# Experts' gate, up and down products of a two-layer decoder in plain fp32 matmuls

## The reference, cut to what matters

```python
def _L1_ffn_ref(hidden_states, gate_w, Wg, Wu, Wd, sg, su, sd):
    ...
    x = hidden_states.reshape(-1, h)
    scores = jax.nn.sigmoid(x @ gate_w.T)
    topk_w, topk_ids = jax.lax.top_k(scores, K)
    topk_w = topk_w / topk_w.sum(-1, keepdims=True)
    comb = jnp.zeros((T, E), dtype=x.dtype).at[jnp.arange(T)[:, None], topk_ids].add(topk_w)
    g = jnp.einsum('th,ehi->tei', x, Wg)
    u = jnp.einsum('th,ehi->tei', x, Wu)
    eo = jnp.einsum('tei,eih->teh', jax.nn.silu(g) * u, Wd)
    routed = jnp.einsum('teh,te->th', eo, comb)
    shared = jax.nn.silu(x @ sg) * (x @ su) @ sd
    return (shared + routed).reshape(b, s, h)
```

## Time and profile before

| what | us |
|---|---|
| runs of the kernel, three | 1480.43, 1484.72, 1488.59; median 1484.72 |
| the profiled execution | 1483.09 |
| its span, first to last instruction | 1481.7 |
| TensorE busy in the span | 1232.3 (83%) |
| VectorE busy | 889.1 (60%) |
| ScalarE busy | 599.9 (40%) |
| GpSimd busy | 327.0 (22%) |

### The profile page before, as it was taken

One profiled execution on the slowest core, in us unless ns is written; L12 is line 12 of the kernel. 1 busy time (PEld: TensorE's weight loads), 2 busy tenths in 40 slices (PEclk: granted clock), 3 DMA queues, 4 the chain that ended last, 5 costly groups with the idle time before them and its releaser, 6 DMA issues.

```text
span 1481.7 us, 19507 instructions
## 1 busy us (share of the span) xinstructions
PE 1232.3 (83%) x7048; PEld 748.6 (51%) x7048; DVE 889.1 (60%) x2091; ACT 599.9 (40%) x1205; POOL 327.0 (22%) x327
## 2 busy tenths in 40 slices
PE   4568868976479934699999899898978999999998
PEld 2234645653336621243335333265544778777777
DVE  3676638575938575767675776177787575542322
ACT  2232146322255621356554465644435343232222
POOL 3410023220443220600000200033321232222222
PEclk9789998985889975799999999999997999999999
DMA  6144530360024300133322020060000000000000
GB/s 180 64 90 93 79 49 1 72 87 1 0 75 86 44 0 0 61 68 44 44 44 44 1 44 2 1 182 1 0 1 1 1 1 15 1 15 1 15 1 15
DMA packets 45919, 56.44 MB, mean 38 GB/s; under 512 B 8742, under 2 KB 30592, under 8 KB 45824
## 3 DMA queue, kind: packets, MB, share of 16 engines
q1 hardware_dynamic: 45824, 55.20, 18.6%
HBM read 40.37 MB, written 14.68 MB: 37 GB/s over the span
## 4 chain that ended last, share of the span: by engine, by line
PE 62%; DVE 22%; ACT 7%; issue 5%; POOL 2%; DMA 2%; SPq 0%; DVEq 0%; ACTq 0%; POOLq 0%
PE psum L923 12%; PE psum L940 7%; PE psum L814 5%; PE psum L602 5%; PE psum L784 4%; PE psum L833 4%; PE psum L684 3%; DVE mx L1639 3%; PE psum L709 2%; PE psum L695 2%; PE psum L503 2%; DVE stats L1254 2%; DVE small L1419 1%; PE psum L584 1%; PE psum L927 1%
## 5 line engine op out<-in xcount | busy, mean ns | idle before, releaser
L1639 DVE TENSOR_REDUCE mx<-psum 128x1 f32<-128x512 f32 (+3 forms) x384 | 200.1, 552 | 87.4 <-PE psum L787 63.1
L1865 POOL TENSOR_TENSOR work<-work,small 128x308 f32<-128x308 f32 x128 | 90.9, 713 | 312.6 <-DVE small L1435 312.6
L923 PE MATMUL psum<-H_r,area_r 128*128 128x512 f32 x408 | 145.6, 398 | 0.0
L1927 POOL TENSOR_TENSOR work_r<-work,work_r 128x512 fp32r<-128x512 f32 x68 | 89.3, 1313 | 250.1 <-ACT work_r L1214 250.1
L784 PE MATMUL psum<-stack_area 96*128 96x512 bf16 (+3 forms) x288 | 100.3, 353 | 45.9 <-DVE mx L1639 44.5
L1766 DVE TENSOR_TENSOR work<-work,psum 128x512 f32<-128x512 f32 x68 | 46.7, 687 | 150.3 <-PE psum L923 148.2
L1155 ACT ACTIVATE work<-psum 128x512 f32<-128x512 f32 (+1 forms) x192 | 94.7, 526 | 78.5 <-PE psum L836 59.9
L684 PE MATMUL psum<-area 128*128 128x308 f32 x256 | 100.7, 479 | 20.1 <-DVE work L1432 15.8
L1214 ACT CAST work_r<-work 128x512 fp32r<-128x512 f32 x68 | 42.2, 620 | 164.3 <-DVE work L1770 157.9
L1155 ACT ACTIVATE HT<-psum 128x384 f32<-128x384 f32 (+2 forms) x192 | 82.4, 454 | 47.6 <-PE psum L836 31.5
L833 PE MATMUL psum<-stack_area 98*128 98x512 bf16 (+3 forms) x288 | 94.9, 336 | 7.1 <-ACT work L1155 3.6
(11 more groups left out here) (254 smaller groups left out, 2721.5 us busy)
## 6 DMA issues: line engine op xcount, KB each, us to landing
stack_area<-parts_a0q SPq DMA_DIRECT2D x24, 128.0 KB, 4.2
stack_area<-parts_a0k SPq DMA_DIRECT2D x24, 128.0 KB, 7.0
stack_area<-parts_a1q SPq DMA_DIRECT2D x24, 128.0 KB, 4.6
stack_area<-parts_a1k SPq DMA_DIRECT2D x24, 128.0 KB, 7.2
stack_area<-parts_d0q SPq DMA_DIRECT2D x18, 128.0 KB, 4.3
stack_area<-parts_d0k SPq DMA_DIRECT2D x18, 128.0 KB, 7.1
stack_area<-parts_d1q SPq DMA_DIRECT2D x18, 128.0 KB, 4.1
stack_area<-parts_d1k SPq DMA_DIRECT2D x18, 128.0 KB, 6.7
```

The costliest lines, as they stand in the source:

```text
L923: done = pe.matmul(u.bank(x), w[:, c, :], h[:, c, cols], start=k == 0, stop=k == len(products) - 1)
L1639: dve.tensor_reduce(mx[:, j, t, half:half + 1], u.bank(k)[:, 0:cols], AX.X, ALU.max).then_inc(*u.empties(k))
L1865: pool.tensor_tensor(ex3, ex3, small[:, of_i + 4:of_i + 8].unsqueeze(2).to_broadcast([P, HPG, CTX]), ALU.mult).then_inc(ctx_prob, 1)
L1927: pool.tensor_tensor(work_r[x % 4][:, :], work[x % 4][:, :], work_r[4 + x % 4][:, :], ALU.subtract).then_inc(act_lo, 1)
```

## The change

Upper and lower parts go away. The gate and up products are one plain fp32 matmul for each half of the contraction, from the unsplit weights and the tokens in `HT`; the down product is one plain fp32 matmul for each tile of 128 tokens, from `work[y % 4]` and the unsplit weight. All three kinds of splits go, on ScalarE, VectorE and GpSimd, with their tiles' second names, their semaphores and the steps in the order of stages.

```diff
-            weave(e["context"](1, "e"), chain(e["context_out"](0, "e"), e["route"](0), e["split_first"]()))
+            weave(e["context"](1, "e"), chain(e["context_out"](0, "e"), e["route"](0)))
...
             def experts(b):
+                pe.wait_ge(*landed["moe"].all())
                 for n in range(SPANS):
...
-                    pe.wait_ge(tokens_lo[b], DC * (n + 1))
                     if n == 0:
+                        for pair in range(TILES // 2):
+                            pe.wait_ge(*u_ln["f", b].empty(pair))
                         pe.wait_ge(sel_done, 1)
...
                     for x in range(NE + DOWN_LAG):
                         if x < NE:
-                            if b == 0 and n == 0:
-                                pe.wait_ge(upper_lo, 3 * (x + 1))
-                            for u, name in ((of_g, "g"), (of_u, "u")):
-                                _, w_hi, w_lo = expert_weights(x, name)
+                            for u, w in ((of_g, wg), (of_u, wu)):
                                 pe.wait_ge(*u.vacant(x))
-                                products = [(w, h, c) for c in range(DC) for w, h in ((w_hi, hx_r[b]), (w_hi, HT_r[b]), (w_lo, hx_r[b]))]
-                                for k, (w, h, c) in enumerate(products):
-                                    done = pe.matmul(u.bank(x), w[:, c, :], h[:, c, cols], start=k == 0, stop=k == len(products) - 1)
+                                for c in range(DC):
+                                    done = pe.matmul(u.bank(x), w[:, c, x, :], HT[b][:, c, cols], start=c == 0, stop=c == DC - 1)
                                 done.then_inc(*u.fills(x))
...
                         if x >= DOWN_LAG:
                             y = x - DOWN_LAG
-                            _, w_hi, w_lo = expert_weights(y, "d")
...
-                            pe.wait_ge(act_lo, first + y + 1)
-                            lo, hi = work_r[y % 4], work_r[4 + y % 4]
+                            pe.wait_ge(*(of_sel.empty(y) if y < EXPERTS else of_u.empty(y)))
                             for q in range(TPS):
-                                obank, o = outs.bank(q // 2), q % 2
-                                for m, (part, w) in enumerate(((hi, w_hi), (hi, w_lo), (lo, w_hi))):
-                                    done = pe.matmul(obank[:, o * D:(o + 1) * D], part[:, q * P:(q + 1) * P], w,
-                                                     start=(y == 0 and o == 0 and m == 0), stop=(y == NE - 1 and m == 2), skip_group_check=True)
+                                done = pe.matmul(outs.bank(q // 2)[:, q % 2 * D:(q % 2 + 1) * D], work[y % 4][:, q * P:(q + 1) * P], down_weights(y),
+                                                 start=(y == 0 and q % 2 == 0), stop=y == NE - 1, skip_group_check=True)
                             done.then_inc(down_done, 1)
...
-                        act.copy(hx_r[b][:, c, cols], HT[b][:, c, cols]).then_inc(tokens_hi[b], 1)
...
-                    act.copy(upper, whole).then_inc(upper_hi, 1)
...
-                            act.activation(s[:, :], of_g.bank(x), ACT.Silu).then_inc(*of_g.empties(x))
-                            act.wait_ge(*(of_sel.empty(x) if x < EXPERTS else of_u.empty(x)))
-                            act.copy(hi[:, :], s[:, :]).then_inc(act_hi, 1)
+                            act.activation(work[x % 4][:, :], of_g.bank(x), ACT.Silu).then_inc(*of_g.empties(x))
...
-                        dve.tensor_tensor(HT_r[b][:, c, cols], HT[b][:, c, cols], hx_r[b][:, c, cols], ALU.subtract).then_inc(tokens_lo[b], 1)
...
-                    dve.tensor_tensor(lower, whole, upper, ALU.subtract).then_inc(upper_lo, 1)
...
-                            pool.wait_ge(act_hi, first + x + 1)
-                            pool.tensor_tensor(work_r[x % 4][:, :], work[x % 4][:, :], work_r[4 + x % 4][:, :], ALU.subtract).then_inc(act_lo, 1)
```

More of the change, by code:

```diff
@@ L186, in sb @@
             return ctx.enter_context(nc.sbuf_tensor(name, shape, dt))
[L188 to L191, removed]
         def sem(name):
@@ L203, in build @@
         X = sb("X", [P, BATCH * TILES, D])
[L204 to L208, removed]
+        H = [sb(f"H{b}", [P, TILES, D]) for b in range(BATCH)]
+        HT = [sb(f"HT{b}", [P, DC, SEQ]) for b in range(BATCH)]
+        stack_area = sb("stack_area", [P, 8192])
+        area = [sb(f"area{b}", [P, 9728]) for b in range(BATCH)]
+        work = [sb(f"work{i}", [P, SPAN]) for i in range(8)]
         W1 = sb("W1", [P, 2048])
-        W2, W2_r = sb2("W2", [P, 2048])
+        W2 = sb("W2", [P, 2048])
         consts = sb("const_tile", [P, KEPT_COLS])
@@ L284, in build @@
                 vx[phase, b] = carve(area[b], at + GROUPS * HPG * CTX, HEADS * STRIP).rearrange("p (h e) -> p h e", h=HEADS)
-        hx, hx_r = [[h[b][:, :, :].rearrange("p t d -> p (t d)").rearrange("p (c t) -> p c t", c=DC) for b in range(BATCH)] for h in (H, H_r)]
+        hx = [H[b][:, :, :].rearrange("p t d -> p (t d)").rearrange("p (c t) -> p c t", c=DC) for b in range(BATCH)]
         ox = [[hx[b][:, 0, :], hx[b][:, 1, :], HT[b][:, 0, :], HT[b][:, 1, :]] for b in range(BATCH)]
@@ L297, in build, with down_weights @@
         w_proj = carve(area[0], 9216, 512).rearrange("p (c n) -> p c n", c=DC)
-        wd_shared, wd_shared_r = [carve(a[0], 8144, D) for a in (area, area_r)]
-        wg, wg_r = [carve(a[0], 3792, DC * NE * INNER).rearrange("p (c e i) -> p c e i", c=DC, e=NE) for a in (area, area_r)]
-        wu, wu_r = [carve(a[1], 3792, DC * NE * INNER).rearrange("p (c e i) -> p c e i", c=DC, e=NE) for a in (area, area_r)]
+        wd_shared = carve(area[0], 8144, D)
+        wg = carve(area[0], 3792, DC * NE * INNER).rearrange("p (c e i) -> p c e i", c=DC, e=NE)
+        wu = carve(area[1], 3792, DC * NE * INNER).rearrange("p (c e i) -> p c e i", c=DC, e=NE)
         sel = carve(area[1], 8144, 1024, BF16).rearrange("p (e n) -> p e n", e=EXPERTS)
[L302 to L316, removed]
+        wd = carve(stack_area, 4096, EXPERTS * D).rearrange("p (e n) -> p e n", e=EXPERTS)
+        def down_weights(x):
+            return wd_shared if x == EXPERTS else wd[:, x, :]
         combt = [carve(area[b], 0, 512, BF16) for b in range(BATCH)]
@@ L385, in build @@
         values_zeroed = sem("values_zeroed")
-        comb_split, sel_done, upper_hi, upper_lo = sem("comb_split"), sem("sel_done"), sem("upper_hi"), sem("upper_lo")
-        tokens_hi, tokens_lo = per_batch("tokens_hi"), per_batch("tokens_lo")
-        act_hi, act_lo, down_done = [sem(f"expert_{n}") for n in ("hi", "lo", "down")]
+        comb_split, sel_done, down_done = sem("comb_split"), sem("sel_done"), sem("expert_down")
         dve_steps, act_steps, pool_steps = Steps(sem("dve_steps")), Steps(sem("act_steps")), Steps(sem("pool_steps"))
@@ L946, in tensor_engine @@
                           context=context, context_out=context_out, spline=spline_layer, attention_inputs=attention_inputs, maxima=maxima,
[L947 removed]
+                          weighted=weighted, masked_inputs=masked_inputs, route=route, experts=experts,
                           between=lambda where: None))
@@ L1179, in route @@
                     yield
-                for n in range(SPANS):
-                    for c in range(DC):
-                        cols = slice(n * SPAN, (n + 1) * SPAN)
-                        act.copy(hx_r[b][:, c, cols], HT[b][:, c, cols]).then_inc(tokens_hi[b], 1)
[L1184 to L1188, removed]
-                    act.copy(upper, whole).then_inc(upper_hi, 1)
[L1191 to L1197, removed]
             def experts(b):
                 for n in range(SPANS):
-                    of_g, of_u, of_sel = u_g[b, n], u_u[b, n], u_sel[b, n]
+                    of_g = u_g[b, n]
                     first = (b * SPANS + n) * NE
@@ L1204, in experts @@
                         if x < NE:
[L1205 to L1208, removed]
                             act.wait_ge(*of_g.full(x))
-                            if k >= 4:
+                            if first + x >= 4:
                                 act.wait_ge(down_done, first + x - 3 if x >= 4 else first)
-                            act.activation(s[:, :], of_g.bank(x), ACT.Silu).then_inc(*of_g.empties(x))
-                            act.wait_ge(*(of_sel.empty(x) if x < EXPERTS else of_u.empty(x)))
-                            act.copy(hi[:, :], s[:, :]).then_inc(act_hi, 1)
+                            act.activation(work[x % 4][:, :], of_g.bank(x), ACT.Silu).then_inc(*of_g.empties(x))
                         yield
@@ L1231, in scalar_engine @@
                           context=context, context_out=context_out, spline=spline_layer, attention_inputs=attention_inputs, maxima=maxima,
-                          weighted=weighted, masked_inputs=masked_inputs, route=route, split_first=split_first, experts=experts,
+                          weighted=weighted, masked_inputs=masked_inputs, route=route, experts=experts,
```

(15 more changed lines are left out.)

24 lines of the change are left out of this document (1 added, 23 removed).

## The result

The changed kernel takes 1545.52 us (median of 4 runs, 1541.04 to 1549.80) against 1482.58 for the kernel before (4 runs, 1476.06 to 1488.59): a ratio of 1.0425, 95% interval 1.0364 to 1.0486, so slower by 4.25%. The profiled execution took 1541.04, its span is 1539.7, 58.0 us more than that of before.

A forecast was written before the change was run, and what follows sets the result against it. TensorE's stream was taken to bound the expert stage; +45.6 + 18.7 - 0.8 - 0.9 - 0.7 = +61.9 us on 1483.1 gave 1545.0, plus 1.6 for the median: 1546 us, range 1534 to 1560.

The forecast's parts named there:

- Gate and up, +0.67 us an iteration: Expert loop: 8 plain records at 0.4275 us replace 12 fp32r matmuls, 2.75 us; over 68 iterations +45.6 us.
- The slow value of 0.4575: Upper price in us of a plain gate or up record, from L864 after another kind of neighbour; would give +61.9 us.
- Down, +0.275: Down product: 8 plain records taking 1.73 us replace 12 fp32r matmuls taking 1.455; over 68 iterations +18.7 us.
- L927's 0.53 us stays: Token-weight matmul in each iteration keeps its 0.53 us, including 0.31 of standstill; bounds -20 to +13 us.
- The small gains: Work taken off ScalarE, VectorE and GpSimd saves only the TensorE waits it caused: -0.8, -0.9 and -0.7 us.
- -0.9: TensorE's wait for VectorE in one iteration while route(1) runs would go, saving 0.9 us.
- -0.7: The last down product's 0.23 us wait for GpSimd's subtraction would go in three spans, saving 0.7 us.
- -0.8: At the start, TensorE's waits of 0.33 and 0.47 us behind ScalarE's token rounding would go, saving at most 0.8 us.
- New waits: Down product now waits for VectorE's last multiplication, 2.0 us after its banks fill; claimed over long before TensorE comes.
- A plain record at the price of a removed matmul (faster): Rival for the expert products: record counts decide, -1.4 us an iteration, -95 us, about 1387 us; chance 0.02.
- The freed engines: Rival of no change: engines relieved of the splits pay the added TensorE time back; chance 0.01.
- The third rival: Each half of a plain record costs what an fp32r matmul costs in the expert products: +95 us, about 1577; chance 0.04.

The follow-up runs named there:

- the kernel with one part: Kernel before with only the upper x upper part of the gate and up products, 8 of 12 fp32r matmuls left out; 1394.90 us against 1479.19, ratio 0.9425.

## Why the prediction was right

**What bounds.** Right. TensorE fills the stage before and after, and 180 us of work on the other engines more or less (the experiment that keeps the splits) leave its length unchanged but for a stretch at half clock.

**Gate and up, +0.67 us an iteration.** Right to 0.04: the experiment with this part alone has +0.635. The price of 0.4275 a record, read from L864 hundreds of microseconds earlier, is 0.430 in the stage. The slow value of 0.4575 did not occur in an undisturbed iteration. The removed matmul was priced a little low, at 0.229 for the 0.233 that the kernel with one part shows, and the net cost so much too high.

**Down, +0.275.** Right: +0.28 to +0.30 alone, and 0.2156 a record against 0.216 from L602. The weight loads stayed covered. Both together give 5.68 - 4.735 = 0.945, the sum of the two terms as predicted; the two experiments add up to 0.92 to 0.93. On top of plain gate and up products the plain down product costs 5.68 - 5.37 = 0.31, so the one term was some 0.035 too high and the other as much too low. That they cancel is luck.

**L927's 0.53 us stays.** Right, and it is no property of the products beside it: beside fp32r and beside plain fp32 alike the step to it is 0.1 longer than the other steps, and the step from it takes 0.32.

**The small gains.** They were rightly small, but partly for another reason than I gave. I put -0.9 and -0.7 to VectorE and GpSimd having less to do. The kernel that keeps every split has neither wait: the longer stream of TensorE covers them. The sum came out right because both reasons remove the same 1.6 us. For the start I allowed at most -0.8. One of the two waits of the earlier trace rows went (0.5 us); the other, 0.33, is still there in the changed kernel at 1133.21. But the whole stretch ahead of the experts is 2.4 us shorter in this pair of traces, and at least 1.1 us shorter without the splits in any pair of this study. So that bound was too small; which instructions give the time back was not traced.

**New waits.** None showed.

**The sum.** +61.9 predicted, +58.0 between the profiled spans, of which +62.7 in the stage and -4.7 ahead of it; +62.9 between the medians. The forecast was 1546 (1545.0 + 1.6 is 1546.6, rounded down), measured 1545.52. The nearness to within a microsecond is luck, since single executions of one kernel differ by 9 to 12 us.

**The rivals.** A plain record at the price of a removed matmul (faster) fell with 0.430 against 0.229. The freed engines do not pay back. A plain matmul is two records of 0.430 us, so four times 0.215 us, and an fp32r matmul of 512 columns took 0.229 to 0.233. The third rival's 16 such matmuls for 12 in each product would have added 95 us, some 32 more than was measured. The Trainium skill (FP8 and Floating Point Precision, TensorE Precision Notes) gives true fp32 four passes through the array. The trace agrees with that in the count, and not in one price for every pass.

**Left open.** Why an fp32r matmul takes 0.229 us for 512 columns and 0.121 for 256, which is about 0.015 more in either case than one column a clock at 2.4 GHz would take (0.213 and 0.107, an estimate), was not tried. Nor where between 64 and 96 rows the border lies, or what in the array makes it.

## What to carry to other kernels

Price a matmul by the distance between starts, and best by the difference of two iterations that differ in one block; the mean duration of a pipelined record said that this change would save time. Three fp32r products cost 0.69 us where one plain fp32 product of 512 columns costs 0.86, so splitting pays on TensorE, as long as the engines that split do not close a ring around it, which was only 0.37 us away. And look for a gap on either side of a matmul with few rows: filling 48 rows up with zeros to 128 took 1.3% off the kernel before. That version, at 1469.56 us against 1488.32, is the fastest complete kernel of this study that was timed more than once; the one with 96 rows took 1461.80 against 1479.29 in single executions.

## What was not expected of the hardware

The matmul of 48 or 64 rows between matmuls of 128 rows costs 0.30 us of standstill, 0.1 before it and the rest behind it (4.735 us an iteration for 4.44); with 96 or 128 rows none is to be seen. Its weight load stands with its own matmul at the same instant (1144.01 in the kernel before, after 0.36 us without a load), where the loads of L923 begin with the matmul before theirs (one at 1142.99, its matmul at the next start, 0.23 us later).

The granted clock fell to half, 1.2 GHz, once in the stage in the profiles of before and after, right behind the 32 narrow matmuls of the routing (16 columns each). Here is the stretch in the kernel before (columns as in the earlier trace rows), and the gate and up block in the chain of the changed kernel:

```profile
1234.00:1237.00 3.00, 3.00 (x9) 2.35 (x8) 0.00 (x0) 1.53 (x2) 0.00 (x0) 0.50 0.00 0
```

```profile
1244.75 5.22 PE psum L895 x8
```

The block takes 5.22 us for the usual 3.43. The kernel with all splits kept ran the same 32 matmuls at a granted clock of 1.00 and is 1.7 us shorter between the two token-weight matmuls around them. So did the kernel with gate and up alone in plain fp32, while the one with the down product alone fell to 0.50 for longer. So this is worth 1.7 us here and comes and goes; TensorE was busy throughout in all of them, and what decides it is not shown.
